# Reordering the group statistics, the filter's base and the tail of a two-stage pre-activation kernel

## The reference

```
a  = gn(x) @ Wa + ba;   b = gn(x) @ Wb + bb;   g = sigmoid(gn(x) @ Wg + bg)
x1 = x + (g * einsum('bijk,bikl->bijl', a, b)) @ Wo + bo
y  = x1 + depthwise_conv(gn(x1), filt)   # 4x4 filter on a 2x dilated image, stride 2
```

## Time and profile before

| | us |
|---|---|
| median of 3 runs | 68.85 (68.38 to 69.01) |
| the profiled execution | 68.02 |
| its span, first to last instruction | 66.2 |
| PE / PEld busy | 50.2 / 37.2 |
| DVE busy | 44.7 |
| POOL busy | 42.3 |
| ACT busy | 30.6 |
| mean granted TensorE clock | 0.903 |

### The profile page before, as it was taken

One profiled execution on the slowest core, in us unless ns is written; L12 is line 12 of the kernel. 1 busy time (PEld: TensorE's weight loads), 2 busy tenths in 40 slices (PEclk: granted clock), 3 DMA queues, 4 the chain that ended last, 5 costly groups with the idle time before them and its releaser, 6 DMA issues.

```text
span 66.2 us, 2441 instructions
## 1 busy us (share of the span) xinstructions
PE 50.2 (76%) x1026; PEld 37.2 (56%) x1026; DVE 44.7 (67%) x123; ACT 30.6 (46%) x52; POOL 42.3 (64%) x52
## 2 busy tenths in 40 slices
PE   3999989876979979998629499867079659999100
PEld 3996967643749848676318178634069552464000
DVE  0092199989646598463999975499964399961750
ACT  5300012444554244956971963996621697423400
POOL 1000419469999999048999978486963719999300
PEclk9999999999999999999999999999995555558965
DMA  0799990000000000000000033100404000040074
GB/s 0 280 233 299 349 354 11 0 10 0 0 10 0 0 10 0 5 10 0 0 10 0 22 136 127 41 10 0 163 0 158 10 0 0 5 158 0 31 286 158
DMA packets 2603, 4.78 MB, mean 72 GB/s; under 512 B 288, under 2 KB 416, under 8 KB 2592
## 3 DMA queue, kind: packets, MB, share of 16 engines
q1 hardware_dynamic: 2592, 4.62, 19.7%
HBM read 2.52 MB, written 2.10 MB: 70 GB/s over the span
## 4 chain that ended last, share of the span: by engine, by line
PE 48%; DVE 26%; issue 6%; ACT 4%; DVEq 0%
PE ps_ag L665 10%; PE ps_ab L610 8%; PE ps_ot L650 7%; DVE x L441 5%; PE ps_ot L577 4%; PE ps_ab L634 4%; DVE zt L434 4%; DVE part L388 4%; PE ps_s L558 3%; DVE bsb L425 3%; PE ps_ag L598 3%; PE ps_ag L622 3%; DVE part L383 2%; PE ps_s L565 2%; ACT gate L305 2%
## 5 line engine op out<-in xcount | busy, mean ns | idle before, releaser
L242 POOL TENSOR_TENSOR y<-y,prod 128x512 f32<-128x512 f32 x12 | 16.5, 1379 | 3.8 <-DVE y L448 3.1
L208 POOL TENSOR_TENSOR rstd<-veps,half 128x2 f32<-128x2 f32 (+1 forms) x7 | 5.6, 802 | 12.6 <-DVE veps L418 12.4
L236 POOL TENSOR_TENSOR xb<-xs,par 128x512 f32<-128x512 f32 x8 | 10.5, 1338 | 1.5 <-issue 1.5
L327 ACT ACTIVATE prod<-x,coef 128x512 f32<-128x512 f32 x12 | 8.2, 712 | 4.4 <-POOL coef L219 4.4
L292 ACT ACTIVATE rt<-ps_ot 128x512 f32<-128x512 f32 x7 | 3.9, 595 | 11.3 <-PE ps_ot L577 11.3
L550 PE MATMUL ps_h<-zeros 128*128 128x128 f32 x46 | 8.2, 346 | 1.0 <-DVE zeros L457 1.0
L550 PEld LDWEIGHTS ps_h<-zeros 128*128 128x128 f32 x46 | 7.5, 252 | 1.0 <-DVE zeros L457 1.0
L448 DVE SCALAR_TENSOR_TENSOR y<-x,coef,y 128x512 f32<-128x512 f32 x6 | 6.7, 1118 | 1.9 <-POOL y L224 1.9
L298 ACT ACTIVATE at<-ps_ag,par 128x512 f32<-128x512 f32 x8 | 5.5, 687 | 5.0 <-PE ps_ag L598 4.8
L305 ACT ACTIVATE gate<-ps_ag,par 128x512 f32<-128x512 f32 x8 | 5.5, 682 | 4.1 <-PE ps_ag L622 4.1
L665 PE MATMUL ps_ag<-x,diag 128*128 128x512 f32 (+4 forms) x12 | 7.0, 719 | 0.0
(11 more groups left out here) (50 smaller groups left out, 80.4 us busy)
## 6 DMA issues: line engine op xcount, KB each, us to landing
xs<-x SPq DMA_DIRECT2D x8, 256.0 KB, 5.2
out<-y SPq DMA_DIRECT2D x8, 256.0 KB, 2.0
par<-params SPq DMA_DIRECT2D x1, 289.5 KB, 4.4
par<-params SPq DMA_DIRECT2D x1, 128.0 KB, 4.1
```

The source lines that it names most:

```text
L236: nc.gpsimd.tensor_tensor(xb[:, w, b, :, :], xs[:, w, b, :, :], bo.broadcast_to([128, ROWS, D]), ALU.add).then_inc(xb_ready, 1)
L242: return nc.gpsimd.tensor_tensor(y[:, w, b, :, :], y[:, w, b, :, :], prod[:, n % 2, k, :, :], ALU.add)
L327: nc.scalar.activation(prod[:, n % 2, k, :, :], x1[:, w, b, 1:ROWS + 1, k:D + k], ACT.Copy, scale=coef[:, w, b, k + 2:k + 3]).then_inc(pro ...
```

## The change

- **Statistics of x1.** `deviation` and both products of jobs 3 to 5 move out of the wave's second unit to the start of the next wave's first unit. On PE that unit is now: `product_a`, step 0, `halo`, `product_b`, step 1, `product_o`. On DVE: `deviation`, `variance`, `b_out`, `x1_out` twice, `filter_right` of image 0, `z_out`. In the second unit DVE does `b_out` first, then `filter_right` of image 1, bn_stats and aggregate of x1, `z_out`.
- **Mean's rows and columns.** The three DVE writes L405 to L407 go. `halo` gets a second, accumulating product, with a weight matrix `bottom` (127 more columns in the parameters), which adds the mean. ACT's `halo_out` is one copy of both images, then the padding column (`pad_ready`), then the mean's term (`nt_ready`, for which POOL's coefficients now wait).
- **Filter base.** That of image 1 is written to PSUM (`ps_f`, shared with the halo) instead of `y`; `filter_right` reads it there.
- **POOL.** `add_bo(3)` is ahead of `filter_coefs(0)`.
- **Tail.** PE: step 0, `halo(2)`, 4 records of idle products, `product_o(3)`, step 1, 12 records of idle products, then the last products with `halo(3)` after the first. DVE and ACT as below; image 0 is finished ahead of image 1, without a second `x1b`.

```diff
 # ACT, end of the list
+            halo_out(LAST - 1)
+            act.wait_ge(x1_ready, 2 * LAST + 1)
+            nc.scalar.activation(y[:, LAST, 0, :, :], x1[:, LAST, 0, 0:ROWS, 0:D], ACT.Copy,
+                                 scale=taps[:, LAST, 0:1]).then_inc(last_base, 1)
             filter_product(LAST - 1, 0, 0)
             filter_product(LAST - 1, 0, 1)
             filter_base1(LAST - 1)
             filter_product(LAST - 1, 1, 0)
+            halo_out(LAST)
             filter_product(LAST - 1, 1, 1)
 # DVE, after the loop over units
-            variance(X1JOB + LAST - 1)
+            deviation(X1JOB + LAST - 1)
             job = X1JOB + LAST
             x1_out(LAST, 0)
+            variance(job - 1)
             x1_out(LAST, 1)
-            filter_right(LAST - 1, 0)
             x1_part(LAST)
             aggregate(job)
-            filter_right(LAST - 1, 1)
+            filter_right(LAST - 1, 0)
             deviation(job)
+            dve.wait_ge(last_base, 1)
             dve.wait_ge(pad_ready, WAVES)
-            dve.wait_ge(last_base, 1)
             last_tap(1)
             variance(job)
+            filter_right(LAST - 1, 1)
             dve.wait_ge(halo_ready, WAVES)
             last_tap(3)
+            dve.wait_ge(last_shift, 1)
+            yw = y[:, LAST, 0, :, :]
+            link(nc.vector.tensor_tensor(yw, yw, prod[:, 0, 0, :, :], ALU.add))
             dve.wait_ge(rstd_done, job + 1)
+            nc.vector.scalar_tensor_tensor(yw, yw, rstd[:, 1, LAST, 0:1], x1[:, LAST, 0, 0:ROWS, 0:D], ALU.mult,
+                                           ALU.add).then_inc(y_dve, 1)
             dve.wait_ge(last_base, 2)
             dve.wait_ge(last_sum, 1)
 # (the same last instruction for image 1 as before)
 # PE, unit loop, first unit of a wave
-                    if g == 2:
-                        stat_product(2, 0)
-                    else:
-                        stat_product(X1JOB + w - 2, 1)
+                    job = 2 if g == 2 else X1JOB + w - 2
+                    stat_product(job, 0)
+                    if w >= 2:
+                        halo(w - 2)
                     product_b(g)
-                    if g == 2:
-                        stat_product(2, 1)
+                    stat_product(job, 1)
                     product_o(w - 1)
```

More of the change, by code:

```diff
@@ L25, in mask_columns @@
     above = (p[:, None] == p[None, :] + 1) & (q[None, :] != 7)
-    last = (q == 7)[:, None]
-    return [m.astype(np.float32) for m in (average, np.eye(128), above, last)]
+    bottom = average * (q == 7)[None, :]
+    return [m.astype(np.float32) for m in (average, np.eye(128), above, bottom)]
 def parameter_columns(Wa, ba, Wb, bb, Wg, bg, Wo, bo, filt):
@@ L191, in _ @@
                     store(w, b)
-            for n, b in enumerate((1, 0)):
-                sp.wait_ge(y_dve, n + 1)
+            for b in range(2):
+                sp.wait_ge(y_dve, b + 1)
                 store(LAST, b)
@@ L267, in _ @@
             normalise(3)
+            add_bo(3)
             filter_coefs(0)
             filter_base(0)
-            add_bo(3)
             add_products(0, 0)
@@ L307, in halo_out @@
             def halo_out(w):
-                act.wait_ge(nmu_ready, w + 1)
                 act.wait_ge(halo_done, w + 1)
[L310 to L314, removed]
+                nc.scalar.activation(x1[:, w, :, ROWS, 0:D], below(w), ACT.Copy).then_inc(halo_ready, 1)
+                act.wait_ge(minus_ready, X1JOB + w + 1)
+                nc.scalar.activation(x1[:, w, :, :, D],
+                                     nmu[:, 1, w, :].rearrange("p (b r) -> p b r", r=1).broadcast_to([128, 2, ROWS + 1]),
+                                     ACT.Copy, scale=-1.0).then_inc(pad_ready, 1)
+                nc.scalar.activation(terms[:, w, :, 4], nmu[:, 1, w, :], ACT.Copy,
+                                     scale=tsum[:, w:w + 1]).then_inc(nt_ready, 1)
             def filter_base1(w):
                 act.wait_ge(coef_ready, w + 1)
-                nc.scalar.activation(y[:, w, 1, :, :], x1[:, w, 1, 0:ROWS, 0:D], ACT.Identity, bias=beta[:, w, 1:2],
-                                     scale=coef[:, w, 1, 0:1]).then_inc(base1_ready, 1)
+                if w >= 1:
+                    act.wait_ge(right_ready, 2 * w)
+                nc.scalar.activation(ps_f[:].rearrange("p (r d) -> p r d", d=D), x1[:, w, 1, 0:ROWS, 0:D], ACT.Identity,
+                                     bias=beta[:, w, 1:2], scale=coef[:, w, 1, 0:1]).then_inc(base1_ready, 1)
             def filter_product(w, b, k):
@@ L336, in _ @@
                     if w >= 2:
+                        halo_out(w - 2)
                         filter_product(w - 2, 0, 0)
@@ L536, in _, with idle_products @@
             nc.vector.scalar_tensor_tensor(y[:, LAST, 1, :, :], ps_ag[:, 0, :].rearrange("p (r d) -> p r d", d=D),
[L537 to L544, removed]
+                                           rstd[:, 1, LAST, 1:2], x1b[:], ALU.mult, ALU.add).then_inc(y_dve, 1)
         @block.tensor
         def _(pe):
-            def idle_products(n, bank=ps_h):
+            def idle_products(n, bank=ps_ab[:, 0, :]):
                 for _ in range(n):
@@ L657, in halo @@
                 pe.wait_ge(x1_ready, 2 * w + 2)
[L658 to L661, removed]
+                pe.wait_ge(to_stat, nth(X1JOB + w, 0))
+                if 1 <= w < LAST:
+                    pe.wait_ge(right_ready, 2 * w)
+                mean = mv[:, 1, w, :, 0].rearrange("p (b d) -> p b d", d=1).broadcast_to([128, 2, D])
+                nc.tensor.matmul(below(w), above, x1[:, w, :, 0, 0:D], start=True, stop=False)
+                nc.tensor.matmul(below(w), bottom, mean, start=False, stop=True).then_inc(halo_done, 1)
             def last_product(k, rows, cols):
@@ L702, in _ @@
                 else:
-                    if w >= 1:
-                        halo(w - 1)
                     product_b(g)
@@ L709, in _ @@
                     product_g(g)
-                    if w >= 1:
-                        stat_product(X1JOB + w - 1, 0)
                     product_ab(g)
+            stat_product(X1JOB + LAST - 1, 0)
+            halo(LAST - 1)
             idle_products(2, ps_ot[:, 0, :])
+            product_o(LAST)
             stat_product(X1JOB + LAST - 1, 1)
-            product_o(LAST)
-            halo(LAST)
+            idle_products(6, ps_ab[:, 0, :])
             every = slice(0, ROWS), slice(0, D)
@@ L722, in _ @@
             stat_product(X1JOB + LAST, 0)
+            halo(LAST)
             last_product(1, slice(0, ROWS), slice(0, D - 1))
```

91 lines of the change are left out of this document (38 added, 53 removed).

## The result

The changed kernel takes 1.0066 times the time of the kernel before, 95% interval 1.0038 to 1.0094: some 0.45 us slower, by this measurement clear of zero and under 1%. The median is 68.50 us over 20 executions, that of the kernel before 69.07 over 20. The changed kernel is the steadier one: 19 of its 20 executions lie between 68.19 and 68.86, those of the kernel before between 67.72 and 70.84 with one at 84.57. The profiled execution took 68.28 us with a span of 66.5 (before: 68.02 and 66.2).

A forecast was written before the change was run, and what follows sets the result against it. The prediction took a chain of waits, not a busy engine, to bound the kernel. Walking the new lists gave span 67.4 against 66.24, +1.2, added to the median 68.85: 70.05, rounded to 70.0 us, own range 69.5 to 70.6.

The forecast's parts named there:

- the difference of the spans in the sum: Whole kernel: span 67.4 forecast against 66.24 in the one profile of the kernel before, +1.2 us.
- Units 4 to 7: Middle units: later coefficients hold the gate, veps 2.79 after product_a(4), product_a(7) at 43.97, z_out(7) done at 48.8 (before 50.32).
- Clock: PE through product_o(3): holds at 2.4 GHz because idling is 1.5 and 1.3, no longer 2.41 in one piece.
- Tail: After unit 7: veps 51.6, filter_right(2,1) done at 58.62 behind last_tap(1), rstd 61.53, last add 63.7, span 67.4.
- the last add: POOL's final add in the tail: ends at 63.7, before 61.92; the last three stores wait for it.
- the signs named: Tail: POOL idle over 1 us before its third add supports the forecast; last store issued before 63.85 speaks against it.
- The turns between VectorE and POOL: Tail: VectorE instructions with two SBUF tensors and POOL ones alternate, whole instruction by whole instruction; sum stays 67.4.
- the rival of cheap turns: Tail: VectorE and POOL interleave without loss, span 65.6 to 66.0, time about 68.5; chance 0.18.
- The start of the sum: Before unit 4: times taken from one profile of the kernel before, product_a(4) at 27.64 instead of 27.88.
- the wider parameters: Parameter load at the start: 127 more columns, 65 kB, 0.2 at the load's rate, counted at nothing as covered.
- Small terms: Unit 3 gains 0.24; in units 4 and 6 the doubled halo takes 0.64, between 0.42 and twice that.
- The median as base: Whole kernel: span difference of +1.2 added to the median 68.85 gives 70.05, rounded to 70.0.

The follow-up runs named there:

- gate_first: Changed kernel with ACT's gate ahead of the two filter products and VectorE's z_out ahead of filter_right of image 0 in units 4 and 6: 0.9890.
- before_idle: Kernel before with 8 idle products (16 records) on PE behind product_g(7), where it waits for the aggregate: 0.9888, span 65.1.
- base_sbuf: Changed kernel with the filter base of image 1 written to y in SBUF, as in the kernel before, instead of PSUM: 1.0164.
- right_early: Changed kernel with filter_right(2,1) on VectorE directly behind deviation of the last job, ahead of last_tap(1) and variance: 0.9866, span 64.7.
- odd_columns: Changed kernel with one more unused parameter column behind bottom, so later tiles start at an odd 4-byte word; no time ratio given, POOL's add of bo 1.28.
- before_width: Kernel before with the last_row parameter column repeated 128 times (65 kB more), only the first column used: 0.9972.

## Why the prediction was wrong

Forecast: +1.2 us, slower by 1.7%, 70.0 us, own range 69.5 to 70.6. Measured: +0.66%, 68.5 us. The direction and the mechanism were right, the size was not: the step that failed is the difference of the spans in the sum, +1.2. Its small terms were 0.4 too long together, which leaves 0.7 at an equal start; and it took the start of one profile as the kernel's, where the changed kernel's profile is 0.47 earlier, so that the two profiles differ by only 0.3.

- **Units 4 to 7: right.** From `product_a(4)` to veps I had 2.79, the trace 2.67; from veps to `product_a(5)` 3.44 and 3.43; on to `product_a(6)` 3.87 and 3.85; to `product_a(7)` 6.23 and 6.10; to the end of z_out(7) 4.83 and 4.80. That the gate waits for the late coefficients was tested by gate_first.
- **Clock: right, with little margin.** It held through `product_o(3)`, and in 19 of the 20 executions the mean clock is 0.944 to 0.959; before_idle shows what the kernel before pays for its fall. But the reason given, no 2.41 of idling in one piece, is not enough by itself: in the profile of gate_first the clock fell after waits of PE of 1.04 and 0.79, in that of base_sbuf after one of 1.10.
- **Tail: right.** From veps of wave 2 to filter_right(2,1) 7.02 and 7.13; to rstd 2.91 and 2.90; to the last add 2.17 and 1.97; to the end of the span 3.7 and 3.8. right_early confirmed the place. Of the signs named, POOL's idling ahead of its third add (1.49) came true; the last store, issued at 63.58, came before the 63.85 that was to speak against the forecast, since everything lay 0.9 earlier. The turns between VectorE and POOL are in the rows (1.63, 1.70, 1.74 beside each other), and with them the exclusive lock of the Trainium skill, SBUF — State Buffer, Who interferes with whom; the rival of cheap turns falls, although its time of 68.5 is the one measured: by this account that is chance. base_sbuf shows the other half of that section: with two SBUF tensors the instruction under a POOL add took 0.83, with one 0.74.
- **The start of the sum: wrong.** I summed against one profile of the kernel before and took its beginning as the kernel's. `product_a(3)` started at 23.66 there and at 23.19 after, 0.47 of difference that lies before the first edit, ahead of the first statistics product, where before waited 0.41 for the masks. The runs show that product at 5.25 to 6.06. I had priced the wider parameters in this place and not asked whether the wait was a fixed one. Span 67.4 forecast, 66.5 found: 0.47 of the 0.9 is this.
- **Small terms: 0.4 too long together.** 0.10 to `product_a(4)`, 0.12 and 0.13 in the two passages over the halo and the statistics, 0.20 at POOL's last add, less 0.11 in the tail. Each came out shorter than forecast. The 0.10 is POOL's shorter adds of bo: with the odd column, where they take 1.28 as before, unit 3 gains the 0.24 of the forecast, without it 0.34; the sum had the wider parameters at nothing. The largest is the last add, put 1.4 behind the end of the VectorE instruction ahead of it, where the rows of before had 1.12 for such a turn, and it measured 1.12.
- **What is left between profile and ratio.** Put at an equal start the two spans differ by 66.5 + 0.47 - 66.24 = 0.7, and the measured ratio says 0.3 to 0.6. The rest is within what the starts scatter from execution to execution. Against the 67.7 that the kernel before has in the three later jobs, the mean of 68.5 is 0.8 longer; which base is the better one is open.
- **The median as base.** 68.85 was a median of three; over 20 executions the kernel before spreads from 67.72 to 70.84 (and one at 84.57). The difference came from a profile of 68.02 and was added to a median 0.83 longer; on the profile's own time the forecast would have been 69.2, and the changed kernel's profile took 68.28.

## What to carry to other kernels

When work is moved on several engines with hand-written orders, walk each list once more for the instruction that stands behind a wait it does not need: here one filter instruction behind a tap on VectorE held POOL, and a gate behind two products on ACT held PE, and undoing the two brought more (2.0 and 1.8 points, each alone) than the whole change moved (0.7). Separate the clock from the order of work by giving the old kernel the same clock; otherwise one hides what the other costs. And before summing against a single profile, see which of its waits lie ahead of the first edit: a wait for a transfer there is not a constant.

## What the hardware showed that was not expected

POOL's add of a row held in SBUF took 1.28 us for 128x512 where the row and the tiles behind the parameters started at an odd 4-byte word of the partition (the kernel before, odd_columns), and 1.09 where they started at an even one (the changed kernel, before_width), whatever the order of work; one unused column is all that odd_columns adds. Whether the start of the row or that of the tiles costs it was not separated. The adds of `y` and `prod` stayed at 1.27 in all of them, so it is not the only condition.
